# A post-norm transformer layer on one core: full-array scores, o moved by DMA, FFN bias on ScalarE, finer waits, another order of steps

## The chip, the cores and the metric

The kernel runs on one core of one Trainium2 chip. The metric is the device time of one execution in microseconds (us); less is better. A core has TensorE (PE; its weight loads are PEld), VectorE (DVE), ScalarE (ACT), GpSimd (POOL) and a queue that only issues DMAs (SP). Each engine works through its own list of instructions in order and waits on semaphores. TensorE's results land in PSUM, in banks of 128 x 512 float32; DMAs move data between HBM and SBUF and within SBUF.

## The reference, cut to what matters

```python
# x: (16, 512, 256) float32, 16 heads of 16, window blocks of 128
qkv = (x @ Wqkv + bqkv).reshape(B, S, 3, H, Dh)
scores = einsum('bhnqd,bhnkd->bhnqk', qb, kwin) / 16     # each block of 128 queries sees 3 blocks of keys
scores = where(|kpos - qpos| <= 128 and in range, scores, -1e30)
out = softmax(scores) @ vwin, reshaped to (B, S, 256)
x = layernorm(x + out @ Wout + bout)
h = relu(x @ quantize(W1).T + b1)                        # 256 -> 1024, weights -1, 0, 1
x = layernorm(x + h @ quantize(W2).T + b2)
```

## The kernel before, in words

A sequence of 512 tokens is one "row" (16 rows). The program walks `row in range(-2, B + 1)`; a step does the attention of row b, the output projection and FFN of row b-1, and the projections of row b+1. Each step has four parts v = 0..3. Part v computes the exponentials of the four heads of quad v of row b, and the row maxima of the quad that comes two parts later (quads 2 and 3 of row b, then 0 and 1 of row b+1).

**Units.** A quad has 12 units of scores and 12 of maxima. Four heads times three units: blocks of 384, of 384, and of two times 256 columns. q and k are split into a high and a low float32r part and stacked by DMAs (`stack`, six DMAs of 128 KB for a quad) into `q_stack` and `k_stack`: quads 0 and 1 lie on partitions 0 to 49, quads 2 and 3 on 64 to 113. So scores (50 partitions) and maxima (48 partitions) of the same part use different halves of the array. Scores go to banks `st_a`, `st_b`, maxima to three banks `mx`. DVE adds the band and takes the maximum (L812), transposes and a DMA bring the negated maximum into `q_stack` as two more rows (step "nmt", L518, L411). ACT takes exp (L670), POOL zeroes the outside of the band (L973, L977).

**Side steps.** The list `SIDE` says, for each part, in which order the rest is issued: "qk" j and "vp" i are projections (L484), "pva" and "pvb" multiply probabilities by v (L503; four heads in four 32-column strips of the array), "ut" transposes the result u (L513) so that DVE can divide by the sums (L848, L852), "ot" transposes it back (L543), "op" is the output projection, "ln1", "x1", "x1t" the first norm and its transpose (L564), "f1" hf p a 256-token piece of FFN 1 (L578 adds the bias as a matmul of 1 with `b1_rows`, L582 the rest), "f2" FFN 2 (L595), "ln2" the second norm, "xs" the split of x, "xr" the residual load. `weave` spreads the units over the side steps by the costs in `COST`, two units at a time (`RUN = 2`, `N_MAX = 3`). `LAG` says by how many maxima DVE puts a side step off.

**Order on SP.** A step begins with the load of x for row b+2 (L381), then `stack(b, 3)` in part 0, `stack(b+1, 0..2)` in parts 1 to 3, the residual load in part 2, `store(b, 0)` in part 3, each part's "nmt" DMA, and `store(b, 1)` at the end. `store` waits for the second norm's scaling on POOL (L1027).

Of the kernel before, what the change touches and what calls it, by code (L numbers as in the profile page):

```python
# [62 lines left out]
]  # L63

COST = {"qk": (3072, 6), "vp": (3072, 12), "op": (3072, 12), "ut": (1024, 4), "ot": (1024, 4), "x1t": (1024, 4),
        "nmt": (256, 1), "f1": (2560, 10), "f2": (8192, 32), "pva": (2200, 1), "pvb": (2200, 1)}
# [4 lines left out]
N_MAX = 3  # L71
# [4 lines left out]
N_SHARED = 6 - N_MAX  # L76

USES_BANK = {"pva", "ut", "qk", "ot", "op", "vp", "x1t", "f1", "f2", "nmt"}
# [20 lines left out]
NEEDS = {"ot": "ut", "op": "ot", "f1": "x1t", "f2": "f1"}  # L99


def weave():

    out = []
    for v in range(QUADS):
        total = sum(COST.get(name_of(s), (0, 0))[0] for s in SIDE[v])
        units = []
        for i in range(UNITS):
            pos = (i // RUN * RUN + RUNS_AT[0]) / UNITS * total * RUNS_AT[1]
            units += [(pos, "scores", i), (pos, "max", i)]  # L110
# [11 lines left out]
WOVEN = weave()  # L122

# [9 lines left out]
def row_of(v, step, at):  # L133
# [9 lines left out]
    if name == "xr":  # L143
        return (0, None) if attn else None
# [17 lines left out]
def dve_order(v):  # L162
# [7 lines left out]
    for step, woven in zip(SIDE[v], WOVEN[v]):  # L170
# [9 lines left out]
        after = late[-1][0] + 1 if late and name_of(late[-1][1]) == name_of(step) in ("ln1", "ln2") else 0  # L180
# [12 lines left out]
def postln_layer(nc, xT, x, wqkv, bqk, bv, wout, bout, w1T, b1, w2T, b2, out):  # L193
    ctx = ExitStack()
    with ctx:
# [11 lines left out]
        B1 = sb("b1_rows", [P, FF], F32R)  # L207
        ONES2 = sb("ones_rows", [P, S // 2], F32R)
# [5 lines left out]
        ONES = sb("ones", [P, P])  # L214
# [5 lines left out]
        SK = sb("k_stack", [P, 8, S], F32R)  # L220
# [4 lines left out]
        RC = sb("recip", [P, TB * 4])  # L225
        ON = sb("o_norm", [P, TB, D])
        OT = [sb("oT_hi", [P, KC, S], F32R), sb("oT_lo", [P, KC, S], F32R)]
        Y = sb("y", [P, TB, D])
        X1 = sb("x1", [P, TB, D])
        X1T = [sb("x1T_hi", [P, KC, S], F32R), sb("x1T_lo", [P, KC, S], F32R)]  # L230
        HID = [sb("hid_hi", [P, FC, S // 2], F32R), sb("hid_lo", [P, FC, S // 2], F32R)]
        RMAX = sb("rmax", [P, 4, NB])
        NMW = sb("neg_max", [P, P])
        NM = NMW[:, 0:8 * NB].rearrange("p (a g n) -> p a g n", a=2, g=4)
        NMT = sb("neg_maxT", [8 * NB, 2, W], F32R)
# [9 lines left out]
        ABS = sb("abs_sums", [P, 3])  # L245
        THR = sb("thresholds", [P, 4])
# [5 lines left out]
        PST = [bank("st_a"), bank("st_b")]  # L252
# [10 lines left out]
        W1RAW = [X1[:, :, :].rearrange(FLAT), ON[:, :, :].rearrange(FLAT)]  # L263
        W2AT = KC * 4 * D
        W2RAW = [PRF[:, W2AT + HALF_W * k:W2AT + HALF_W * (k + 1)] for k in range(2)]
        B1R = PRF[0:1, W2AT + 2 * HALF_W:W2AT + 2 * HALF_W + FF]
# [8 lines left out]
        s_small = sem("bqk_bv_in")  # L275
        s_const = sem("constants")
# [4 lines left out]
        s_b1 = sem("b1_lo_in")  # L281
# [28 lines left out]
        s_utf = sem("uT_full")  # L310
        s_rc = sem("recip_done")
        s_on = sem("o_norm_done")
        s_otf = sem("oT_full")
# [9 lines left out]
        s_rs1 = sem("ln1_rstd_done")  # L323
        s_nmr = sem("neg_mean_rstd")
        s_x1 = sem("x1_done")
# [13 lines left out]
        s_od = sem("out_stored")  # L339
# [5 lines left out]
        def _(sp):  # L345
# [5 lines left out]
            def more_weights():  # L351
# [5 lines left out]
                sp.dma_start(B1R, b1[None, :]).then_inc(s_wo, 16)  # L357
# [3 lines left out]
            def stack(r, v, first):  # L361
# [4 lines left out]
                sp.wait_ge(s_qkl, 4 * r + 2 * c + 2)  # L366
                if not first:
                    sp.wait_ge(s_stf, 12 * (4 * r - 4 + v) + 12)
                half = slice(64 * ih, 64 * ih + 64)
                heads = slice(4 * ih, 4 * ih + 4)  # L370
                for dst, j, terms in ((SQ, 2 * c, (0, 1, 0)), (SK, 2 * c + 1, (0, 0, 1))):
                    for t, part in enumerate(terms):
                        rows = slice(64 * c + 16 * t, 64 * c + 16 * t + 16)
                        sp.dma_start(dst[rows, heads, :].bitcast(F32), QK[j][part][half, :].bitcast(F32)).then_inc(s_stk[v], 16)

            def step(b, at):
# [9 lines left out]
                if at == 0:  # L386

                    sp.wait_ge(s_wsplit_l, 3)
                    sp.dma_start(B1[1:2, :].bitcast(F32), Y[0:1, :, :].rearrange("p t d -> p (t d)")) \
                        .then_inc(s_b1, 16)  # L390
                for v in range(QUADS):
# [6 lines left out]
                    if v == 2 and attn:  # L398
                        if at == 0:
                            sp.wait_ge(s_b1, 16)  # L400
                        else:
                            sp.wait_ge(s_x1, 4 * b)
# [3 lines left out]
                    if q is not None:  # L406
                        r, vq = b + q[0], q[1]
                        sp.wait_ge(s_nmt, 4 * r + vq + 1)
                        c, ih = vq // 2, vq % 2
                        rows = SQ[64 * c + 48:64 * c + 50, 4 * ih:4 * ih + 4, :].bitcast(F32)  # L410
                        sp.dma_start(rows.rearrange("a g (n q) -> a (g n) q", n=NB), NMT[:, vq % 2].bitcast(F32)).then_inc(s_nmin[vq], 16)  # L411
                if post:
                    store(b, 1)
# [222 lines left out]
        def _(act):  # L636
# [36 lines left out]
            def side_work(v, step, b, dr, vq, at):  # L673
# [408 lines left out]
```

## Time and profile before

| what | value |
|---|---|
| time, median of 3 runs | 1185.28 us (1185.11 to 1187.25) |
| the profiled execution: its own time, its span | 1187.86 us, 1186.1 us |
| mean granted TensorE clock | 0.924 |
| busy share of PE, DVE, ACT, POOL | 89%, 72%, 52%, 44% |
| one row in the steady part (589.17 to 657.44) | 68.27 us |

The span is the time from the first to the last instruction of the profiled execution; what lies around it is 1.8 us. A row repeats from about 112 us to 1067 us, from the part in which the first attention row starts to the last row that still prepares another.

### The profile page before, as it was taken

The page shows a single profiled execution, that of the slowest core. Times are in us where ns is not written, and L with a number is a line of the kernel's source. Part 1 is how long each engine was busy: PE and PEld are TensorE (multiplying, and loading weights), DVE is VectorE, ACT ScalarE, POOL GpSimd, SP SyncE. Part 2 cuts the span into 40 slices and gives each one's busy share as a digit, 9 for nine tenths or more (in the row PEclk, how much of TensorE's full clock was granted, in tenths as well). Part 3 has the DMA queues.
Part 4 walks back from the last instruction along what each step waited for, and adds up shares of the span by engine and source line. Part 5 has one row for each costly group of instructions (what it writes and reads, how often), then busy time and mean ns, then how long its engine had stood idle before and what let it go on. Part 6 is the DMA issues. An engine that isn't in the chain of part 4 may idle for free.

```text
span 1186.1 us, 23520 instructions
## 1 busy us (share of the span) xinstructions
PE 1056.2 (89%) x8132; PEld 771.9 (65%) x8132; DVE 859.3 (72%) x2934; ACT 613.3 (52%) x1258; POOL 518.8 (44%) x824
## 2 busy tenths in 40 slices
PE   4778899999989899998989999898989999897966
PEld 3444676766767576676767666676767667675755
DVE  3975777778787777778777777877777787777333
ACT  4154554655455564556455555545655554555421
POOL 2124353544535445463535445453535445344430
PEclk9677899998989999898999989898998989898889
DMA  5835255434354443444344534424554342442000
GB/s 169 108 54 92 28 82 82 68 70 73 58 75 68 83 73 76 61 80 65 56 82 73 88 61 78 75 37 82 82 82 68 69 74 57 57 69 56 1 19 18
DMA packets 56999, 81.49 MB, mean 69 GB/s; under 512 B 7729, under 2 KB 27697, under 8 KB 56882
## 3 DMA queue, kind: packets, MB, share of 16 engines
q1 hardware_dynamic: 56882, 80.00, 40.3%
q8 instruction: 66, 1.08, 0.4%
q14 instruction: 51, 0.42, 0.2%
HBM read 20.19 MB, written 8.39 MB: 24 GB/s over the span
## 4 chain that ended last, share of the span: by engine, by line
PE 77%; DVE 13%; issue 4%; POOL 2%; ACT 2%; DMA 1%; SPq 0%; POOLq 0%; DVEq 0%; ACTq 0%
PE shared L484 18%; PE st_a L459 13%; PE shared L503 12%; PE shared L595 11%; PE shared L582 10%; DVE mx L812 5%; PE st_b L459 5%; PE shared L578 3%; PE shared L564 3%; DVE oT_lo L859 2%; POOL ln_rstd L1007 1%; PE shared L543 1%; PE mx L475 1%; DVE qk_lo L839 1%; DVE rmax L812 1%
## 5 line engine op out<-in xcount | busy, mean ns | idle before, releaser
L812 DVE CUSTOM_DVE_ANT_0 mx<-mx,band 128x384 f32<-128x384 f32 (+1 forms) x1024 | 480.1, 514 | 187.0 <-PE mx L475 182.6
L670 ACT ACTIVATE probs<-st_a 128x384 f32<-128x384 f32 (+1 forms) x384 | 202.0, 526 | 371.3 <-PE st_a L459 367.7
L475 PE MATMUL mx<-k_stack,q_stack 48*128 48x384 f32 (+1 forms) x1024 | 273.0, 369 | 8.0 <-DMA k_stack<-qk_lo 3.9
L973 POOL TENSOR_SCALAR_AFFINE_SELECT probs<-probs 128x512 f32<-128x512 f32 (+1 forms) x256 | 128.8, 527 | 317.5 <-ACT probs L670 316.3
L670 ACT ACTIVATE probs<-st_b 128x384 f32<-128x384 f32 (+1 forms) x384 | 200.8, 523 | 0.0
L459 PE MATMUL st_a<-q_stack,k_stack 50*128 50x384 f32 (+1 forms) x512 | 186.9, 406 | 3.1 <-ACT probs L670 2.4
L475 PEld LDWEIGHTS mx<-k_stack,q_stack 48*128 48x128 f32 x1024 | 165.7, 201 | 13.2 <-DVE rmax L812 8.7
L503 PE MATMUL shared<-probs,v_aug 128*32 128x384 f32 (+1 forms) x2048 | 161.2, 445 | 0.7 <-DVE x L902 0.7
L459 PEld LDWEIGHTS st_a<-q_stack,k_stack 50*128 50x128 f32 x512 | 90.3, 197 | 104.2 <-issue 63.5
L812 DVE DVE_READ_ACCUMULATOR2_ANT rmax<- 128x1 f32 x1024 | 144.5, 141 | 0.0
L459 PE MATMUL st_b<-q_stack,k_stack 50*128 50x384 f32 (+1 forms) x512 | 143.2, 320 | 0.0
L582 PE MATMUL shared<-x1T_hi,w1q 128*128 128x256 f32 x512 | 142.9, 295 | 0.0
L582 PE MATMUL shared<-x1T_lo,w1q 128*128 128x256 f32 x512 | 138.5, 288 | 0.0
L595 PE MATMUL shared<-w2q,hid_hi 128*128 128x256 f32 x512 | 131.9, 293 | 4.1 <-DVE hid_lo L895 4.1
L595 PE MATMUL shared<-w2q,hid_lo 128*128 128x256 f32 x512 | 131.8, 293 | 0.0
L977 POOL TENSOR_SCALAR_AFFINE_SELECT probs<-probs 128x512 f32<-128x512 f32 (+1 forms) x256 | 127.1, 520 | 0.0
L895 DVE SCALAR_TENSOR_TENSOR hid_lo<-shared,hid_hi 128x512 fp32r<-128x512 f32 x128 | 87.9, 687 | 36.0 <-ACT hid_hi L740 34.6
L740 ACT ACTIVATE hid_hi<-shared 128x512 fp32r<-128x512 f32 x128 | 76.8, 600 | 59.4 <-PE shared L582 59.4
L595 PEld LDWEIGHTS shared<-w2q,hid_hi 128*128 128x128 f32 x512 | 97.7, 191 | 14.7 <-issue 10.2
L582 PEld LDWEIGHTS shared<-x1T_hi,w1q 128*128 128x128 f32 x512 | 99.4, 194 | 10.5 <-issue 7.7
L503 PEld LDWEIGHTS shared<-probs,v_aug 128*32 128x32 f32 x2048 | 57.7, 111 | 68.2 <-issue 50.7
L595 PEld LDWEIGHTS shared<-w2q,hid_lo 128*128 128x128 f32 x512 | 97.4, 190 | 6.9 <-issue 2.9
(107 smaller groups left out, 1965.3 us busy)
## 6 DMA issues: line engine op xcount, KB each, us to landing
q_stack<-qk_hi SPq DMA_DIRECT2D x128, 128.0 KB, 4.3
k_stack<-qk_hi SPq DMA_DIRECT2D x128, 128.0 KB, 5.2
x_raw<-in_xT SPq DMA_DIRECT2D x16, 512.0 KB, 5.7
q_stack<-qk_lo SPq DMA_DIRECT2D x64, 128.0 KB, 3.9
k_stack<-qk_lo SPq DMA_DIRECT2D x64, 128.0 KB, 5.5
y<-in_x SPq DMA_DIRECT2D x16, 512.0 KB, 6.1
out<-x SPq DMA_DIRECT2D x32, 256.0 KB, 2.1
probs<-in_w2T SPq DMA_DIRECT2D x1, 1024.0 KB, 10.6
```

Of the source, the lines that this page charges most:

```text
L459: mm = pe.matmul(PST[i % 2][:, col:col + n], SK[rows, hd, W * m:W * m + W], SQ[rows, hd, q0:q0 + n], start=True, stop=True)
L475: mm = pe.matmul(PMX[i % N_MAX][:, col:col + n], SQ[rows, hd, W * m:W * m + W], SK[rows, hd, k0:k0 + n], start=True, stop=True)
L484: mm = pe.matmul(ps, lhs(a, kc), rhs(z, kc), start=(n == 0), stop=(n == len(terms) - 1))
L503: mm = pe.matmul(G[32 * g:32 * g + 32, q0:q0 + width], VAUG[:, vq, m, g, :], PR[:, vq % 2, g // 2, lo:lo + width], start=(m == 0), stop=(m ...
L582: mm = pe.matmul(ps, W1Q[:, kc, P * f:P * f + P], X1T[a][:, kc, 256 * hf:256 * hf + 256], start=False, stop=(kc == KC - 1 and a == 1))
L595: mm = pe.matmul(G[:, D * t:D * t + D], HID[a][:, f, P * t:P * t + P], W2Q[:, f, :], start=(f == 0 and a == 0), stop=(f == FC - 1 and a == 1))
L670: act.activation(PR[:, v % 2, g // 2, lo:lo + n], PST[i % 2][:, 0:n], ACT.Exp, scale=SCALE) \
L740: act.activation(HID[0][:, 2 * p:2 * p + 2, :].rearrange("p f t -> p (f t)"), G[:, :], ACT.Relu).then_inc(s_hh, 1)
L812: mx = dve.tensor_tensor_reduce(ps, ps, band, 1.0, -3e38, ALU.add, ALU.max, RMAX[:, g, m:m + 1])
L895: dve.scalar_tensor_tensor(pair[1], G[:, :], 0.0, pair[0].bitcast(F32), ALU.max, ALU.subtract).then_inc(s_hl, 1)
L973: pool.affine_select(out=pr_before, in_=pr_before, compare_op=ALU.is_ge, fill=0.0, base=0, pattern=[[0, n], [1, W]], channel_multiplier=-1)
L977: last = pool.affine_select(out=pr_after, in_=pr_after, compare_op=ALU.is_ge, fill=0.0, base=0, pattern=[[0, n], [-1, W]], channel_multipl ...
```

## The change

- **Scores and maxima use the whole array.** `k_stack` becomes two tensors, one for quads 0 and 1 and one for 2 and 3, each zero in the other half's partitions; `q_stack` is shared. Scores multiply 128 partitions, maxima 112. The two rows of ones and the negated maximum move to partitions 124 to 127. A `stack` now waits also for the maxima of two quads earlier, and scores for the stack of the quad two later. `BANKS = (2, 3)` gives two banks for scores and three for maxima, as before; the "nmt" transpose (72 columns of output) uses a bank of the maxima.
- **o goes to columns by DMA.** "ut" and "ot" on TensorE go. v is interleaved with ones, so that u holds o on even and the sum on odd partitions. `columns`, two DMAs of 128 KB for a quad, bring them apart into `o_cols` and `sums_cols`; step "od" takes the reciprocal of 128x512 sums and multiplies (half 0: reciprocal on DVE, product on POOL; half 1: both on DVE). "ot" is then the split of `o_cols` on ACT and DVE.
- **FFN bias on ScalarE.** The matmul L578 goes. ACT applies bias and relu in two 256-column instructions to `u` or `hidden` (by turns), then copies to float32r; DVE or, for p = 1, POOL subtracts.
- **Waits.** op, x1t, f1 and f2 wait for the half, tile or pair that they need, the first norm's scale is computed for two tiles at a time, x1 tiles 0 and 2 are on DVE, 1 and 3 on ACT.
- **Order.** A new `SIDE`, new costs, single units instead of pairs, and some ACT steps ahead of the exponentials of their step.

```diff
 SIDE = [
-    [("qk", 0), "nmt", "pva", "pvb", ("vp", 0), "ut", ("vp", 1), ("ot", 0), ("ot", 1), ("qk", 1), ("op", 0),
-     ("op", 1)],
-    [("ln1", 0), ("ln1", 1), ("ln1", 2), ("qk", 2), "nmt", ("ln1", 3), "pva", "pvb", ("x1", 0), ("x1", 1),
-     ("x1", 2), ("x1", 3), "ut", ("x1t", 0), ("x1t", 1), ("qk", 3), ("f1", 0, 0)],
...
+    [("ot", 0), ("qk", 0), ("qk", 1), "pva", "pvb", "nmt", ("vp", 0), ("qk", 2), ("od", 1)],
+    [("qk", 3), ("ot", 1), ("vp", 1), ("op", 0), ("ln1", 0), ("ln1", 1), ("op", 1), ("ln1", 2), ("ln1", 3), "nmt",
+     ("x1", 0), ("x1", 1), ("x1", 2), "pva", "pvb", ("xs", 0), ("x1", 3), ("x1t", 0), ("x1t", 1), ("f1", 0, 0),
+     ("f1", 0, 1)],
+    [("f1", 0, 2), ("f1", 0, 3), "pva", "pvb", "nmt", ("f2", 0)],
+    [("xs", 1), ("f1", 1, 0), "nmt", "xr", ("ln2", 0), ("f1", 1, 1), ("ln2", 1), ("f1", 1, 2), ("f1", 1, 3),
+     ("od", 0), "pva", "pvb", ("f2", 1), ("ln2", 2), ("ln2", 3)],
 ]
-RUN = 2
-RUNS_AT = (0.5, 0.92)
-LAG = {"ln1": 1, "ln2": 1, "qk": 1, "ot": 1, "x1t": 0, "f1": 0, "op": 1, "ut": 0, "f2": 1}
+BANKS = (2, 3)
+N_SCORE, N_MAX = BANKS
+REST_ON_POOL = (1,)
+X1_ON_DVE = (0, 2)
+LAG = {"ln1": 1, "ln2": 0, "qk": 0, "od": 3, "ot": 0, "x1t": 0, "f1": 2, "op": 0, "f2": 1}
...
             def scores(b, v, i, at):
-                rows = slice(64 * c, 64 * c + 50)
                 if i == 0:
                     pe.wait_ge(s_stk[v], 96 * b + 96)
                     pe.wait_ge(s_nmin[v], 16 * b + 16)
+                    if v < 2 or stages(at)[2]:
+                        pe.wait_ge(s_stk[(v + 2) % 4], 96 * (b + v // 2) + 96)
...
-                    mm = pe.matmul(PST[i % 2][:, col:col + n], SK[rows, hd, W * m:W * m + W],
-                                   SQ[rows, hd, q0:q0 + n], start=True, stop=True)
+                    mm = pe.matmul(PST[i % N_SCORE][:, col:col + n], SK[c][:, hd, W * m:W * m + W],
+                                   SQ[:, hd, q0:q0 + n], start=True, stop=True)
...
+            def columns(r, vq):
+                i, q = vq // 2, 4 * r + vq
+                rows = slice(64 * (vq % 2), 64 * (vq % 2) + 64)
+                sp.wait_ge(s_u, q + 1)
...
+                sp.dma_start(OC[rows, i, :], U[0:P:2, :]).then_inc(s_uin, 16)
+                sp.dma_start(SC[rows, :], U[1:P:2, :]).then_inc(s_uin, 16)
...
+                elif name == "od":
+                    i = step[1]
+                    dve.wait_ge(s_uin, 128 * r + 64 * i + 64)
+                    dve.reciprocal(SC[:, :], SC[:, :]).then_inc(s_rc, 1)
+                    if i == 1:
+                        dve.wait_ge(s_rc, 2 * r + 2)
+                        dve.tensor_tensor(OC[:, i, :], OC[:, i, :], SC[:, :], ALU.mult).then_inc(s_od, 1)
...
-                        pe.matmul(ps, B1[:, P * f:P * f + P], ONES2[:, :], start=True, stop=False)
...
+                    if p % 2 == 0:
+                        act.wait_ge(s_uin, 32 * min(4 * b + v - (SIDE[v].index(step) < SIDE[v].index("pvb")), 4 * B))
+                    if n > 1:
+                        act.wait_ge(*rest_done(n - 2))
+                    for k, f in enumerate((2 * p, 2 * p + 1)):
+                        last = act.activation(H[:, 256 * k:256 * k + 256], G[:, 256 * k:256 * k + 256], ACT.Relu,
+                                              bias=B1C[:, f:f + 1])
+                    last.then_inc(s_hr, 1)
+                    act.wait_ge(s_hr, n + 1)
+                    act.activation(HID[0][:, 2 * p:2 * p + 2, :].rearrange("p f t -> p (f t)"), H[:, :],
+                                   ACT.Identity).then_inc(s_hh, 1)
```

## Rows read from the trace of the kernel before

**Rows 1.** The page: span, busy time (share of the span) of the engines.

```profile
span 1186.1 us, 23520 instructions
PE 1056.2 (89%) x8132; PEld 771.9 (65%) x8132; DVE 859.3 (72%) x2934; ACT 613.3 (52%) x1258; POOL 518.8 (44%) x824
```

**Rows 2.** Windows: length, busy of PE, PEld, DVE, ACT, POOL, clock, DMA share, GB/s.

```profile
589.17:657.44 68.27, 63.51 (x511) 46.67 (x510) 52.61 (x183) 37.73 (x78) 32.50 (x52) 0.95 0.40 72
...
615.00:617.00 2.00, 0.74 (x5) 0.44 (x5) 1.57 (x9) 1.12 (x3) 1.02 (x2) 1.00 0.02 1
617.00:619.00 2.00, 0.60 (x5) 0.31 (x3) 1.76 (x7) 1.18 (x3) 1.85 (x6) 0.69 0.00 0
619.00:621.00 2.00, 1.94 (x9) 1.65 (x11) 0.76 (x4) 1.26 (x3) 0.77 (x2) 0.50 0.00 0
```

**Rows 3.** Waits in one row's length (560 to 628 us): total, times, longest.

```profile
PE shared L564 <- ACT x L727: 1.5, 1, 1.5
PE shared L513 <- ACT u L714: 1.4, 1, 1.4
...
PE shared L484 <- DVE o_norm L852: 1.0, 1, 1.0
...
PE shared L484 <- DVE oT_lo L859: 0.6, 1, 0.6
```

**Rows 4.** Timeline of PE: runs of units in FFN 2 and at part 1, nmt, pv.

```profile
586.71 0.28 PE L595 MATMUL shared<-w2q,hid_hi 128*128 128x256 f32 x1
586.92 0.44 PE L459 MATMUL st_a<-q_stack,k_stack 50*128 50x384 f32 x1
586.92 0.44 PE L475 MATMUL mx<-k_stack,q_stack 48*128 48x384 f32 x1
...
587.75 0.28 PE L595 MATMUL shared<-w2q,hid_hi 128*128 128x256 f32 x1
...
592.76 0.39 PE L484 MATMUL shared<-xT_lo,wqkv_hi 128*128 128x512 f32 x1
592.99 0.27 PE L518 MATMUL shared<-identity,neg_max 128*128 128x128 f32 x1
593.20 1.28 PE L503 MATMUL shared<-probs,v_aug 128*32 128x256 f32 x16
...
609.26 0.44 PE L459 MATMUL st_a<-q_stack,k_stack 50*128 50x384 f32 x1
```

**Rows 5.** Pieces of the chain that ended last (start, length).

```profile
560.52 0.12 PE shared L578
...
601.55 0.87 PE shared L543 x8
```

**Rows 6.** Timeline of DVE, then of POOL, from the end of FFN 2.

```profile
589.38 0.68 DVE L902 TENSOR_TENSOR x<-shared,x 128x512 f32<-128x512 f32 x1
589.98 0.24 DVE L848 RECIPROCAL recip<-shared 128x16 f32<-128x16 f32 x1
...
590.60 0.74 DVE L910 BATCH_NORM_STATS2 ln_stats<-x 128x6 f32<-128x256 f32 x2
...
591.66 0.19 POOL L1020 TENSOR_SCALAR var_eps<-ln_mv 128x2 f32<-128x2 f32 x1 [1.28 <-DVE ln_mv L913]
591.93 0.72 POOL L1022 TENSOR_TENSOR ln_rstd<-var_eps,minus_half 128x2 f32<-128x2 f32 x1
592.76 2.43 POOL L1027 TENSOR_SCALAR x<-x,ln_mv,ln_rstd 128x256 f32<-128x256 f32 x2
```

**Rows 7.** Timeline of SP's issues, then DMA sizes and time to landing.

```profile
595.22 0.39 SPq L417 DMA_DIRECT2D out<-x  x1
...
599.55 0.67 SPq L374 DMA_DIRECT2D k_stack<-qk_lo  x1
...
k_stack<-qk_lo SPq DMA_DIRECT2D x1, 128.0 KB, 6.6
...
k_stack<-qk_lo SPq DMA_DIRECT2D x1, 128.0 KB, 5.0
```

More of the change, by code:

```diff
@@ L106, in weave @@
         total = sum(COST.get(name_of(s), (0, 0))[0] for s in SIDE[v])
[L107 to L110, printed above, removed]
+        units = [((i + SCORES_AT[0]) / UNITS * total * SCORES_AT[1], "scores", i) for i in range(UNITS)]
+        units += [((i + MAXIMA_AT[0]) / UNITS * total * MAXIMA_AT[1], "max", i) for i in range(UNITS)]
+        units.sort()
         at, slot = 0, []
@@ L122, with units_before, ffn_steps_in_u @@
 WOVEN = weave()
+def units_before(v, step, kind):
+    return sum(k == kind for woven in WOVEN[v][:SIDE[v].index(step)] for _, k, _ in woven)
+NMT_AT = [units_before(v, "nmt", "max") for v in range(QUADS)]
+assert max(NMT_AT) < UNITS
+def ffn_steps_in_u():
+    out, n, last = [], 0, 0
+    for v in range(QUADS):
+        for step in SIDE[v]:
+            if name_of(step) == "f1":
+                n += 1
+                last = n if step[2] % 2 == 0 else last
+            if step == "pvb":
+                out.append(last)
+    return out
+U_FFN = ffn_steps_in_u()
 def stages(at):
@@ L213, in postln_layer @@
         IDN = sb("identity", [P, P])
[L214 removed]
+        ONES = ONES2[:, :].bitcast(F32)
         BAND = sb("band", [P, 3 * W])
@@ L466, in max_scores @@
                 c, hd = v // 2, 4 * (v % 2) + g
-                rows = slice(64 * c, 64 * c + 48)
+                rows = slice(0, 112)
                 if i == 0:
@@ L471, in max_scores @@
                     pe.wait_ge(s_mxr, 12 * (4 * r + v) + i - N_MAX + 1)
+                if i == NMT_AT[(v + 2) % 4] and not (first and v == 0):
+                    pe.wait_ge(s_nmt, 4 * r + v)
                 for m in BLOCKS[u]:
@@ L483, in split3 @@
                     passed()
+                    if chunk is not None and n % 3 == 0:
+                        chunk(kc)
                     mm = pe.matmul(ps, lhs(a, kc), rhs(z, kc), start=(n == 0), stop=(n == len(terms) - 1))
@@ L751, in step @@
                             other_weights()
+                        row = row_of(v, step, at)
+                        before = name_of(step) in ("nmt", "ot", "pvb", "x1")
+                        if row is not None and before:
+                            side_work(v, step, b, *row, at)
                         for _, kind, i in woven:
@@ L754, in step @@
                                 exp(b, v, i, at)
-                        row = row_of(v, step, at)
-                        if row is not None:
+                        if row is not None and not before:
                             side_work(v, step, b, *row, at)
@@ L871, in side_work @@
                         dve.wait_ge(s_mv2, 4 * r)
-                        dve.wait_ge(s_x1, 4 * r)
+                        for t in range(TB):
+                            dve.wait_ge(*x1_done(r - 1, t))
                     t = step[1]
@@ L890, in side_work @@
                         .then_inc(s_x1l, 1)
-                elif name == "f1":
+                elif name == "f1" and step[2] not in REST_ON_POOL:
                     hf, p = step[1], step[2]
@@ L959, in _ @@
             pool.memset(ONES2[:, :].bitcast(F32), 1.0).then_inc(s_const, 1)
-            pool.memset(B1[:, :].bitcast(F32), 0.0).then_inc(s_const, 1)
-            pool.memset(SK[:, :, :].bitcast(F32), 1.0).then_inc(s_const, 1)
+            for half in SK:
+                pool.memset(half[:, :, :].bitcast(F32), 0.0).then_inc(s_const, 1)
             pool.wait_ge(s_const, CONSTANTS)
```

296 lines of the change are left out of this document (156 added, 140 removed), and 4 rows, old and new, of the table SIDE.

## The prediction

> **What bounds the kernel now.** I read the page first: PE is busy for 89% of the span and the next engine, DVE, for 72% [rows 1]. Then the windows, cut to one row in the steady part: of 68.27 us PE works 63.51 and DVE 52.61, so neither is full, and for some 6.8 us of each row the clock is at its lower level, 1.2 instead of 2.4 GHz [rows 2] (the slice from 617 us has 0.69 of full speed, the one from 619 has 0.50, and it stays so until nearly 625). Then the waits, to see what PE's 4.8 idle us of a row are: 1.5 for x1, 1.4 for u, 1.0 for o_norm, 0.6 for oT_lo [rows 3], the rest small. The clock falls just after the wait for x1, where PE was busy 0.74 and 0.60 of 2 us [rows 2]. PE then worked about 5.4 us at half speed, which cost 2.7 us. So a row is PE work at full clock of 60.8 us, idle time of 4.8 and 2.7 of low clock. PE bounds the kernel, and the waits that count are the ones that end on it.
>
> **PE's work.** *Scores and maxima.* A row has 24 runs of two units. From the last FFN matmul ahead of a run to the second one behind it 1.04 us pass (586.71 to 587.75) [rows 4], two of them the usual 0.12 apart: 0.80 us for the run. It starts each score matmul at the time of its twin for the maxima, so a run pays once for two matmuls. But its 896 columns, at the 0.118 us that an FFN matmul of 256 takes, are 0.41 us of it; 0.39 us go into the passage from full-array matmuls to these and back. A transpose (L518) among full-array matmuls costs no such gap (592.99 is 0.23 behind 592.76), the column strips of L503 behind it do (593.20, 0.21 later where the transpose needs 0.11) [rows 4]: the gap belongs to the change of tile, not to a wait. 24 runs at 0.80 to 0.85 (the latter where a unit of 384 columns follows another) are 19.2 to 20.4; I take 19.6 us. In the full array nothing is doubled and nothing switches: 0.118 us for 256 columns and 0.233 for 512 [rows 4], halfway 0.175 for 384; four blocks, twice, for 16 heads are 18.7 us. So -0.9 us.
> The Trainium skill (TensorE: Matmul & The Clock Gate, Part 3: Packing small matmuls) says that small matmuls in distinct row groups run together and that this is the gain to go for; by that rule alone the change would double 9.35 us a row. It also says (TensorEngine Tiling (Array Packing), Key Properties) that a change of tiling mode drains the array, and the trace's 0.39 us a run agrees.
> *Bias.* 16 matmuls of 0.118 [rows 5]: -1.9. *u and o transposes.* 16 and 8 of 0.109 (0.87 for eight) [rows 5]: -2.6. Together PE's work falls by 5.4 us a row. I keep -5.4; the least is -4.4 (no gain on the units, u's transposes partly in the shadow of the switch), the most -6.4.
>
> **PE's idle time.** The waits for u, o_norm and oT_lo go (3.0 us): the path of o has qk 2, qk 3 and vp 1 in front of it. Two places remain or are new.
> *The start of part 1.* Call S the end of f2 (589.17). The last stack of q and k for a row, quad 3, is issued in part 0 and needed by the first unit of part 1. Its path is not touched: z at S+0.2; its 0.60, then norm statistics, now without the division between them (-0.62); POOL from var_eps to the end of the scaling 3.5 us [rows 6]; so the store is issued at S+5.4 instead of 6.05, then x, six stack transfers, the last at S+9.8, landing 6.6 us later [rows 7]: S+16.4. Now PE comes there at S+20.1 (609.26) [rows 4]. After the change part 0 has no op, vp 1, ut and ot: three qk (18 at 0.233, 4.2), vp 0 (12 at 0.118, 1.4), two halves of pv (1.28 each [rows 4] and their borders, 2.8), nmt 0.1, a quarter of 18.7: 13.2 us, so PE arrives at S+13.4 and waits 3.0 us. If the transfers land as fast as those of the emptier queue (5.0 us [rows 7]) it is 1.4; with the negated maximum's DMA landing 1.5 us behind, 4.5. Then "od" 1: `columns` is issued after it (SP needs 0.67 us for an issue [rows 7]), lands at about S+17.8, DVE stands at the head of its queue until then, with every later maximum behind it, and takes 1.3 us for reciprocal and product (a 128x512 operation is 0.60 apart, as L902 [rows 6]; bounds 0.5 to 1.5 each). The first maximum is then read at S+19.6; the fourth, which needs its bank, is due at S+19.9: no wait.
> *x1.* Call T the end of op 1. y 0.6, statistics 1.0, POOL 0.2+0.3+0.7+0.2 with the steps between, then ACT with u, an exp and xs 0 ahead in its queue: the last tile of x1 is there at T+5.4. PE has pv, three unit pairs and three transposes, to T+4.4: 1.0 idle. Then x1T's halves with nothing behind them (qk 3 stood there before): ACT 0.6 and DVE 0.7, 1.3 idle. Together 2.3 instead of 1.5. Bounds 1 and 4.
> With 0.6 for small ones (now 0.3) idle is 5.9: +1.1.
>
> **Clock.** The fall now at x1 costs 2.7. x1's wait becomes two shorter ones with work between; the wait at part 1 is one of 3.0 us, longer than the one that today precedes the fall. I take one low stretch, moved to part 1: 0. Bounds: none (-2.7), both (+2.7).
>
> **Beside the path.** ACT: 8 times two 256-column relus instead of one of 512, a wait for itself and a copy, +0.7 each, to 43.5 of 64 us. DVE: without ut (2.7) and one of four 128x512 subtractions (1.2), with two reciprocals and a product (1.9), 50.5. POOL +4, to 37. SP: 8 issues more, 5 us of a row. All have room on average; what they delay is in the rivals. In the prologue the memset of a second k_stack ends before the first qk input; the tail gains 2 us of bias and loses as much in transfers for o. Row 15 has no maxima beside its scores and waits for the same stack: no change.
>
> **Sum.** -5.4 + 1.1 + 0 = -4.3 us a row; 15 rows (-1 to 14 count as 15 whole ones): -65. The profiled span of 1186.1 becomes 1121, its execution 1123; the median lay 2.6 below the profiled execution, so **1121**.
>
> **Rivals.**
> (a) *Both low stretches.* The two short waits of x1 (2.3 us within 2.9) bring the clock down as well: +2.7 a row, 1162. For it: the slices before today's fall were busy for a third only [rows 2]; mine would be so for 2.9 us. Together with a landing 1.5 us later it reaches 1183.
> (b) *No wait at part 1.* If the six transfers land by S+14.5 or PE is later than I count, the wait shrinks below a microsecond and the clock stays up there: -2 to -3 for the wait, -2.7 for the clock, 1040 to 1095. Against it: these transfers share the engines with x (512 KB).
> (c) *Slower: transfers of u.* `columns` adds 1 MB of SBUF traffic a row, in the queue behind the stack. Where "od" 1 waits on DVE, each microsecond that it lands after S+18 is one that all maxima and PE's banks wait. It must be 4.5 us later, S+22.3, to eat the gain, and then slower with (a): 1190 to 1215. Against it: DMA engines are used for 40% of the row [rows 2].
> (d) *Slower: the rule of row groups.* If the 0.39 us of a run stay (each single unit still pays for something at its borders) while the twins come apart, 24 x 0.39 = 9.4 us a row more than counted: 1262. The transpose without a gap [rows 4] speaks against it. This is what the skill's rule on row groups would bring.
> (e) *Nothing.* Idle time grows by what PE's work loses: 1183 to 1188.
>
> **Numbers.** Forecast (1095 to 1145) 0.38; (a) 1145 to 1183 0.20; (b) 0.27; (c) 0.08; (d) 0.04; (e) 0.03. 0.2% is about what a measurement of this kernel can tell from no change. Faster is the forecast, (a) and (b), 0.85; same 0.03; slower 0.12. The range from 1045 to 1183 leaves out 0.07 below and 0.13 above; the forecast's own is 1095 to 1145.
>
> **What would show it.** Right: in steady rows score and maxima matmuls of 128 and 112 rows about 0.175 apart, units with no gap at their borders, a row of 64 us, PE waiting for a stack or a maximum at the first unit of part 1 for 3 us, the low clock behind it, DVE idle ahead of the reciprocal, x1's wait split in two. Wrong: full clock throughout and a row under 60 us (b), two low stretches (a), PE waiting for DVE's maxima in part 1 (c), units dearer than 0.8 us for two pairs (d). Most doubtful is the arrival time at part 1: it sets the wait and the clock together.

## The result

The changed kernel takes 1277.53 us (median of 4 runs, 1275.92 to 1282.52), the kernel before beside it 1186.26 us (4 runs, 1185.11 to 1187.25): ratio 1.0777, 95% interval 1.0744 to 1.0809. It is 7.8% slower; I had forecast 1121 us and a range from 1045 to 1183.

The page of the changed kernel: span and busy times, then the chain that ended last, by engine and by line.

```profile
span 1275.8 us, 23049 instructions
PE 1055.8 (83%) x7492; PEld 842.3 (66%) x7492; DVE 940.1 (74%) x2821; ACT 736.4 (58%) x1513; POOL 630.1 (49%) x936
...
PE 47%; DVE 20%; DMA 11%; ACT 7%; issue 7%; SPq 7%; POOL 1%; DVEq 0%; POOLq 0%; ACTq 0%
```

PE has 640 matmuls less than before and is as long busy as before [rows 1], in a longer span. Less than half of the chain is PE's; DVE has 20% and transfers 11%.

One row in the steady part, then windows of 2 us at three places (columns as in [rows 2]).

```profile
573.00:648.40 75.40, 64.27 (x468) 51.70 (x468) 56.49 (x174) 45.53 (x94) 39.40 (x58) 0.95 0.45 78
...
618.00:620.00 2.00, 0.32 (x1) 0.32 (x2) 2.00 (x8) 0.00 (x0) 1.05 (x1) 0.94 0.00 0
620.00:622.00 2.00, 2.00 (x11) 2.00 (x11) 1.77 (x10) 0.88 (x2) 0.42 (x2) 0.50 0.18 66
...
640.00:642.00 2.00, 0.00 (x0) 0.00 (x0) 0.00 (x0) 0.00 (x0) 0.00 (x0) 1.00 1.15 139
...
644.00:646.00 2.00, 2.00 (x8) 1.72 (x7) 0.92 (x1) 0.54 (x3) 0.00 (x0) 0.50 1.08 121
...
650.00:652.00 2.00, 2.00 (x11) 1.81 (x11) 2.00 (x7) 1.38 (x3) 0.00 (x0) 0.62 0.01 4
652.00:654.00 2.00, 2.00 (x11) 2.00 (x11) 1.29 (x6) 0.49 (x1) 0.00 (x0) 0.53 0.03 8
```

A row is 75.40 us where 68.27 were [rows 2] and 64 were forecast. It has two low stretches of the clock (0.50 in the windows from 620 and from 644), each behind a stop of PE: from 618 to 620 PE is busy for 0.32 us while DVE works throughout, from 640 to 642 no engine works at all, while the DMA engines are full. Just behind this row, after another stop of PE, the clock is low again (0.62 and 0.53 in the last two windows).

Waits of that row (total, times, longest), which answer to [rows 3].

```profile
PEld mx L546 <- DVE rmax L888: 6.7, 8, 2.0
...
PE mx L546 <- DMA k_stack_bottom<-qk_lo: 3.8, 1, 3.8
...
PE mx L546 <- DVE rmax L888: 2.9, 3, 1.8
...
PE mx L546 <- ACT neg_maxT L768: 1.8, 2, 1.1
...
PE shared L642 <- DVE oT_x1T_lo L959: 1.1, 1, 1.1
...
PE shared L628 <- ACT x L791: 0.6, 1, 0.6
...
PE shared L557 <- DVE oT_x1T_lo L928: 0.4, 1, 0.4
```

The waits for u and o_norm are gone, the one for the split of o (L928) is 0.4 and the one for x1 is 0.6. In their place PE waits for the stack of quad 3 and, in weight loads and matmuls, for DVE to read maxima.

PE's timeline in part 3 and at the start of part 1, then DVE's (start, length, operation, in brackets the idle time before it).

```profile
615.60 0.28 PE L656 MATMUL shared<-w2q,hid_hi 128*128 128x256 f32 x1
615.71 0.34 PE L546 MATMUL mx<-k_stack_top,q_stack 112*128 112x384 f32 x1
615.88 0.34 PE L528 MATMUL st<-q_stack,k_stack_bottom 128*128 128x384 f32 x1
616.06 0.28 PE L656 MATMUL shared<-w2q,hid_lo 128*128 128x256 f32 x1
...
617.60 0.28 PE L656 MATMUL shared<-w2q,hid_lo 128*128 128x256 f32 x1
619.68 0.77 PE L546 MATMUL mx<-k_stack_top,q_stack 112*128 112x256 f32 x2 [1.80 <-DVE rmax L888]
...
638.19 0.40 PE L557 MATMUL shared<-xT_hi,wqkv_hi 128*128 128x512 f32 x1
642.43 0.44 PE L546 MATMUL mx<-k_stack_bottom,q_stack 112*128 112x384 f32 x1 [3.84 <-DMA k_stack_bottom<-qk_lo]
...
649.75 0.44 PE L546 MATMUL mx<-k_stack_bottom,q_stack 112*128 112x384 f32 x1 [1.72 <-DVE rmax L888]
```

```profile
615.51 3.35 DVE L921 RECIPROCAL sums_cols<-sums_cols 128x512 f32<-128x512 f32 x1
618.78 0.41 DVE L888 CUSTOM_DVE_ANT_0 mx<-mx,band 128x256 f32<-128x256 f32 x1
...
645.08 3.35 DVE L921 RECIPROCAL sums_cols<-sums_cols 128x512 f32<-128x512 f32 x1 [1.12 <-DMA sums_cols<-u]
648.47 0.69 DVE L924 TENSOR_TENSOR o_cols<-o_cols,sums_cols 128x512 f32<-128x512 f32 x1
649.08 0.56 DVE L888 CUSTOM_DVE_ANT_0 mx<-mx,band 128x384 f32<-128x384 f32 x1
```

The reciprocal over 128x512 takes 3.35 us, in both halves of o (x32, 107.2 us in all). I had put 0.6 on it. Its neighbour, a product of the same shape, takes 0.69. While the reciprocal runs no maximum is read, PE fills its three banks and stops: at 617.88 (until 619.68), and in part 1 at 648.03 (until 649.75).

SP's issues around the start of part 1, then the time from issue to landing in that window, which answer to [rows 7].

```profile
629.51 0.38 SPq L485 DMA_DIRECT2D out<-x  x1
629.93 0.47 SPq L433 DMA_DIRECT2D x_raw<-in_xT  x1
630.56 0.61 SPq L426 DMA_DIRECT2D q_stack<-qk_hi  x1
...
633.77 0.63 SPq L426 DMA_DIRECT2D k_stack_bottom<-qk_lo  x1
...
635.91 0.60 SPq L481 DMA_DIRECT2D sums_cols<-u  x1
...
k_stack_bottom<-qk_lo SPq DMA_DIRECT2D x1, 128.0 KB, 8.6
...
sums_cols<-u SPq DMA_DIRECT2D x1, 128.0 KB, 9.1
```

The last stack transfer lands 8.6 us after its issue, at 642.4, and the sums at 645.06, 9.1 after theirs. The same transfers for quad 2 take 5.5 us, those of the sums in the other parts 2.9 (medians over the rows). Here x, the stack, the columns of u and the next stack follow each other within 11 us.

### The profile page after: what moved, and what is told of

Same layout as the page of the kernel before. It is cut to its first block, busy times and chain, and to the rows that moved or that the text cites. A ratio compares the mean times of both kernels' runs of the same rounds, so it can differ in the third digit from the quotient of the medians.

```text
span 1275.8 us, 23049 instructions
## 1 busy us (share of the span) xinstructions
PE 1055.8 (83%) x7492; PEld 842.3 (66%) x7492; DVE 940.1 (74%) x2821; ACT 736.4 (58%) x1513; POOL 630.1 (49%) x936
## 3 DMA queue, kind: packets, MB, share of 16 engines
q1 hardware_dynamic: 68136, 96.84, 43.2%
## 4 chain that ended last, share of the span: by engine, by line
PE 47%; DVE 20%; DMA 11%; ACT 7%; issue 7%; SPq 7%; POOL 1%; DVEq 0%; POOLq 0%; ACTq 0%
PE shared L576 11%; DMA sums_cols<-u 9%; PE mx L546 9%; DVE sums_cols L921 8%; PE shared L642 8%; PE st L528 7%; PE shared L656 6%; PE shared L557 6%; DVE mx L888 5%; SPq L426 4%; ACT u L811 2%; DVE oT_x1T_lo L928 1%; ACT hidden L811 1%; DVE x L972 1%; ACT u L776 1%
## 5 line engine op out<-in xcount | busy, mean ns | idle before, releaser
L730 ACT ACTIVATE probs<-st 128x384 f32<-128x384 f32 (+1 forms) x768 | 394.1, 523 | 317.8 <-PE st L528 314.6
L546 PE MATMUL mx<-k_stack_bottom,q_stack 112*128 112x384 f32 (+1 forms) x512 | 162.3, 359 | 90.4 <-DMA k_stack_bottom<-qk_lo 49.2
L546 PE MATMUL mx<-k_stack_top,q_stack 112*128 112x384 f32 (+1 forms) x512 | 153.3, 346 | 52.2 <-DVE rmax L888 31.4
L642 PE MATMUL shared<-oT_x1T_hi,w1q 128*128 128x256 f32 x512 | 140.2, 296 | 16.7 <-DVE oT_x1T_lo L959 16.0
L528 PE MATMUL st<-q_stack,k_stack_top 128*128 128x384 f32 (+1 forms) x512 | 150.6, 336 | 3.3 <-DMA q_stack<-neg_maxT 2.5
L528 PE MATMUL st<-q_stack,k_stack_bottom 128*128 128x384 f32 (+1 forms) x512 | 144.5, 323 | 3.3 <-ACT probs L730 2.0
L642 PE MATMUL shared<-oT_x1T_lo,w1q 128*128 128x256 f32 x512 | 139.6, 292 | 0.0
L921 DVE RECIPROCAL sums_cols<-sums_cols 128x512 f32<-128x512 f32 x32 | 107.2, 3349 | 25.0 <-DMA sums_cols<-u 25.0
L642 PEld LDWEIGHTS shared<-oT_x1T_hi,w1q 128*128 128x128 f32 x512 | 102.6, 200 | 20.5 <-issue 20.5
L528 PEld LDWEIGHTS st<-q_stack,k_stack_top 128*128 128x128 f32 x512 | 97.2, 209 | 10.7 <-issue 7.0
L642 PEld LDWEIGHTS shared<-oT_x1T_lo,w1q 128*128 128x128 f32 x512 | 102.9, 201 | 0.0
```

Of the source, the lines that this page charges most:

```text
L528: mm = pe.matmul(PST[i % N_SCORE][:, col:col + n], SK[c][:, hd, W * m:W * m + W], SQ[:, hd, q0:q0 + n], start=True, stop=True)
L546: mm = pe.matmul(PMX[i % N_MAX][:, col:col + n], SQ[rows, hd, W * m:W * m + W], SK[c][rows, hd, k0:k0 + n], start=True, stop=True)
L642: mm = pe.matmul(G[:, 256 * k:256 * k + 256], W1Q[:, kc, P * f:P * f + P], X1T[a][:, kc, 256 * hf:256 * hf + 256], start=(kc == 0 and a == ...
L730: act.activation(PR[:, v % 2, g // 2, lo:lo + n], PST[i % N_SCORE][:, 0:n], ACT.Exp, scale=SCALE) \
L921: dve.reciprocal(SC[:, :], SC[:, :]).then_inc(s_rc, 1)
```

## Experiments

Each time is the median beside runs of the kernel before on the same chip (1185.5 to 1187.9 us there); differences are against 1277.5 us unless another kernel is named. "A row" is a sixteenth.

### The reciprocal and the place of the stack

**No reciprocal.**
```diff
-dve.reciprocal(SC[:, :], SC[:, :]).then_inc(s_rc, 1)
+dve.tensor_scalar(SC[:, :], SC[:, :], 1.0, None, ALU.mult).then_inc(s_rc, 1)
```


> The changed kernel with each 128x512 reciprocal on DVE (3.35 us, two a row) replaced by a multiplication by 1.0 in the same place. It leaves the reciprocal out: o is multiplied by the sums instead of being divided by them. Theory A (the reciprocal was priced at 0.6 us and takes 3.35; it stands in DVE's queue ahead of the maxima, once for each half of o, and PE waits for both): if the replacement takes about 0.55 us, 2.8 us go from each of two places a row, 16 rows, 90 us: 1188 us, with 1170 to 1215 as the bounds. Theory B (the landing of the last transfers decides the start of part 1, and the reciprocal mostly fills time in which PE waits anyway): no more than one of the two places gives something back, at most 45 us, 1232 or above.

Measured: 1202.7 us (ratio to before 1.0134, 1.0100 to 1.0169), 75 us less, 4.7 a row for 5.4 us of DVE work taken away (the multiplication takes 0.43 us at the end of part 0, but 0.86 in part 3). Theory A's range held; B fell. It is still slower than before, so the reciprocal isn't all.

**One half at a time**, the same edit for `i == 0` or `i == 1` alone.

> The changed kernel, with the reciprocal of the first half of o alone (in part 3) replaced by the multiplication by 1.0; this leaves that reciprocal out. With both replaced 75 us went. If the two places cost alike, 1240 us (1230 to 1250). If the place at the end of part 0 carries it (there PE first waits for the stack, then for the maxima behind the reciprocal), 1260 us or more here and 1215 or less in the run beside it; if part 3 carries it, the reverse.

> The same for the second half of o alone (end of part 0). Two places that cost alike: 1240 us (1230 to 1250). The place at the end of part 0 alone: 1215 us or less. The place in part 3 alone: 1260 us or more, since the wait for the stack and for the transfers of u is still there.

Measured: 1230.5 us without the one in part 3 (47 us less), 1247.0 without the one at the end of part 0 (31 less). Both lie within the bounds of "alike" (1230 to 1250), at its two ends, and the executions of the two kernels do not overlap (1228 to 1234 and 1239 to 1251). So both reciprocals are on the path, and together they make 78, the 75 of both. The one that my forecast never put on the path, in part 3, is the dearer, although less DVE work went there.

**Stack first.** In SP's queue the stack of quad 3 goes ahead of the store and of x:
```diff
 attn, post, nxt, nxt2 = stages(at)
+if attn:
+    stack(b, 3, at == 0)
+if at >= 2:
+    store(b - 1, 1)
 if nxt2:
...
-    if v == 0 and attn:
-        stack(b, 3, at == 0)
...
-if post:
+if at == B:
     store(b, 1)
```


> The changed kernel with one order changed in SP's queue: the stack of quad 3 is issued first in a step, ahead of the store of the second half of the row before and of the load of x. Reciprocals stay. In the profile of the changed kernel PE waits 3.8 us for this stack at the start of part 1 and the transfers of u behind it land 9.2 us after their issue. The stack can now be issued about 5 us earlier. Theory A (the reciprocal decides): the wait for the stack goes, but DVE still stands before the transfers of u and then 3.35 us in the reciprocal; at most the 3.8 us are given back in each of 15 rows, so 1220 to 1277 us, with 1240 as the likeliest. Theory B (transfers decide): both the stack and the transfers of u land 4 us or more earlier, 1200 us or below.

Measured: 1226.3 us (1.0322, 1.0302 to 1.0342), 51 us less, within theory A's bounds; theory B fell. PE's wait for this stack, 49.2 us over all rows, is 0.5. Its wait for maxima is what is left:

```profile
PEld mx L548 <- DVE rmax L890: 140.5, 143, 5.0
...
PE mx L548 <- DVE rmax L890: 74.8, 45, 4.8
```

**x behind the stack, the store still in front**, to see which of the two held it up:
```diff
+if attn:
+    stack(b, 3, at == 0)
 if nxt2:
```
(and the line in the loop removed, the store unchanged at the end of a step).

> The changed kernel with only the load of x (512 KB) moved behind the stack of quad 3 in SP's queue; the store stays in front, and SP waits there for the end of the second norm. Theory T1 (the load of x shares the DMA engines with the stack, whose last transfer took 8.6 us to land): the landing comes down to 5 or 6 us, about 3 us a row, 1225 to 1240 us, nearly all that the stack first brought. Theory T2 (the wait for the store, until 5.4 us into the part, sets the landing): only the issue of x, 0.7 us a row, is gained, 1262 to 1277 us.

Measured: 1261.0 us, 16.5 less, just beyond T2's range and far from T1's. The landing did what T1 said: the last stack transfer took 5.5 us (median over the rows) instead of 8.1, and with x behind the stack PE's wait for it fell from 49.2 to 7.2 us. But the transfers behind it now share with x: the sums still take 6.7 us to land at this place (8.6 before), and 26 us of wait for the negated maximum (2.5 before) took a good part of the stack's place. The rest of the 51 us, 35, came only with the store behind the stack too.

**Both edits**, no reciprocal and stack first.

> Both edits of the two runs before together: the multiplication by 1.0 in the place of the reciprocal (the reciprocal is left out) and the stack of quad 3 issued first in a step. If the two costs are the two terms by which the forecast of 1121 us was wrong, and nothing else was, this run should come to about that: 90 us for the reciprocals and 40 to 55 for the stack from 1277, 1130 to 1150 us. If it stays above 1180, something else that neither theory names holds at least 2 us of each row.

Measured: 1123.4 us (0.9456, 0.9431 to 0.9480), 154 us less than the changed kernel and 5.4% faster than before, 7 us below the range expected. Together the two edits give more than the sum of their own runs (75 + 51): with one cost gone, part of its time goes into waits for the other (PE's wait for maxima rose from 61.4 to 74.8 us with the stack first, its wait for the stack from 49.2 to 51.9 without the reciprocals). Without these two costs the change is a gain, so nothing else is needed to explain the loss.

### Can the reciprocal be hidden on DVE?

```diff
-    [("ot", 0), ("qk", 0), ("qk", 1), "pva", "pvb", "nmt", ("vp", 0), ("qk", 2), ("od", 1)],
-    [("qk", 3), ("ot", 1), ("vp", 1),
+    [("ot", 0), ("qk", 0), ("qk", 1), "pva", "pvb", "nmt", ("vp", 0), ("qk", 2)],
+    [("od", 1), ("qk", 3), ("vp", 1), ("ot", 1),
...
-    [("xs", 1), ("f1", 1, 0), "nmt", "xr", ("ln2", 0), ("f1", 1, 1), ("ln2", 1), ("f1", 1, 2), ("f1", 1, 3),
-     ("od", 0), "pva",
+    [("xs", 1), ("f1", 1, 0), "nmt", "xr", ("ln2", 0), ("od", 0), ("f1", 1, 1), ("ln2", 1), ("f1", 1, 2), ("f1", 1, 3),
+     "pva",
...
+cols = slice(S // RECIPS * k, S // RECIPS * (k + 1))
+dve.reciprocal(SC[:, cols], SC[:, cols]).then_inc(s_rc, 1)
```
with the stack first, `RECIPS` 4 in one run and 1 in the other.

> The order of the last pair of runs (the stack of quad 3 first in a step) with the true reciprocal, cut into four pieces of 128 columns that stand in DVE's queue with a maximum between two of them: for the first half of o in part 3 from the statistics on, for the second half at the start of part 1 instead of the end of part 0. Theory A (what costs is how long a single block keeps the maxima from being read, PE having three banks for them): a piece is about 0.85 us, less than the banks give, so the 103 us between the run with the stack first (1226) and the one without reciprocals (1123) come back but for a few: 1125 to 1155 us. Theory C (what costs is DVE's total, 5.8 us more a row on an engine that is busy for 52.5 of 65 us): the time stays near 1226 us, 1195 or above.

> The same places in DVE's queue as the run before, but each reciprocal whole (128x512, 3.35 us) instead of in four pieces. Theory A (length of the block against three banks): maxima come about 1.3 us apart, so PE waits some 1.5 to 2.5 us in each of two places a row, 1165 to 1215 us. Theory P (only the old places were bad, the end of part 0 above all): within 10 us of the run with four pieces.

Measured: 1279.4 us in quarters and 1239.9 whole. Theory A fell in both runs and P in the second; of C only the bound (1195 or above) held, not the 1226 itself. Finer pieces were the slower. Waits of the kernel in quarters, over all rows:

```profile
PE shared L563 <- DVE oT_x1T_lo L938: 81.5, 16, 11.5
...
ACT hidden L817 <- POOL hid_lo L1098: 52.7, 15, 3.5
...
PE st L534 <- ACT probs L736: 43.7, 26, 3.5
```

PE no longer stops for maxima, but for what the later reciprocal delays: op waits about 4.6 us of a steady row for the second half of o, and POOL, which waits at the head of its queue for the sums of the first half (52.6 us over all rows, 26.3 in the changed kernel), holds back hid_lo, which ScalarE waits for, and so the exponentials. Four pieces also cost more than one (128 of 0.935 us, 118 us, for 107). At the start of part 1 DVE has no room: in the run with both edits it works from 569.74 to 578.7 with hardly a gap.

**Off DVE.** Stack first, and ScalarE makes the reciprocal:
```diff
+act.preload_act_table_set("natural_log_exp_and_others")
...
+act.wait_ge(s_uin, 128 * r + 64 * i + 64)
+act.activation(SC[:, :], SC[:, :], ACT.Ln).then_inc(s_ln, 1)
+act.wait_ge(s_ln, 2 * r + i + 1)
+act.activation(SC[:, :], SC[:, :], ACT.Exp, scale=-1.0).then_inc(s_rc, 1)
...
-dve.wait_ge(s_uin, 128 * r + 64 * i + 64)
-dve.reciprocal(SC[:, :], SC[:, :]).then_inc(s_rc, 1)
```


> The stack of quad 3 first in a step, and the reciprocal of the sums taken off DVE: ScalarE computes exp(-ln(s)) in its place, two 128x512 activations of about 0.6 us for each half of o, with both functions in the one table set that is loaded at the start. Theory A' (the two runs before showed that a piece at the start of part 1 or in part 3 costs wherever DVE, or a helper that waits for it, has no slack; what counts is that these 6.7 us leave DVE at those places): this should come near the run without reciprocals (1123 us), 1125 to 1145. Rival: ScalarE stands at the head of its queue for the transfers of u and then 1.2 us in the two activations, PE has only two banks for scores, and two such waits a row cost 1 to 2 us each: 1150 to 1190 us.

Measured: 1128.3 us (0.9512, 0.9488 to 0.9537), as theory A' had it. It beats both kernels, by 4.9% and 11.7%. One row of it, its waits in that row, and the new instructions:

```profile
565.00:630.00 65.00, 60.53 (x476) 48.89 (x472) 51.43 (x174) 47.10 (x99) 39.36 (x59) 1.00 0.51 94
```

```profile
PE mx L549 <- ACT neg_maxT L772: 1.8, 2, 1.1
PE shared L645 <- DVE oT_x1T_lo L967: 1.1, 1, 1.1
PE shared L631 <- ACT x L801: 0.6, 1, 0.6
PE mx L549 <- DVE rmax L898: 0.2, 1, 0.2
PE st L531 <- ACT probs L734: 0.2, 1, 0.2
PE shared L560 <- DVE oT_x1T_lo L936: 0.2, 1, 0.2
```

```profile
L786 ACT ACTIVATE sums_cols<-sums_cols 128x512 f32<-128x512 f32 x32 | 20.2, 632 | 1.0
L784 ACT ACTIVATE sums_cols<-sums_cols 128x512 f32<-128x512 f32 x32 | 19.8, 619 | 8.5 <-DMA sums_cols<-u 8.5
...
L701 ACT ACT_TABLE_LOAD x1 | 1.3, 1283 | 0.8 <-PEq L1164 0.8
```

0.62 and 0.63 us instead of 3.35, on an engine with room, and no wait in a row is over 1.1 us, so the clock stays up. The Trainium skill (ScalarE: Activation LUTs, Table sets: the hidden batching unit) says that one set holds exp and ln together; the single table load agrees.

### The terms of PE's work

**Maxima in a row group.**
```diff
-rows = slice(0, 112)
+rows = slice(64 * c, 64 * c + 48)
```


> The changed kernel with the maxima's matmuls cut to the 48 rows of one half of the array (what they leave out are rows that hold zeros, so the result is unchanged), while the scores keep all 128 rows. Each unit of maxima is then a passage from the full array to another tile and back, with no twin that could share it. By the step of my forecast that put 0.39 us on such a passage in the kernel before, 48 units a row cost up to 18.7 us more a row where PE is not waiting, up to 280 us in all, and at least a half of that where PE's waits hide some: 1400 to 1560 us. If the change of tile costs nothing and the kernel before lost its 0.39 us to something else, the time stays at 1277 us.

Measured: 1483.2 us in a single execution, 206 more, 12.9 a row or 0.27 for each of 48 passages, within the range expected. In FFN 2 of this kernel a pair of units and its borders:

```profile
644.00 0.28 PE L656 MATMUL shared<-w2q,hid_hi 128*128 128x256 f32 x1
644.21 0.44 PE L546 MATMUL mx<-k_stack_top,q_stack 48*128 48x384 f32 x1
644.58 0.44 PE L528 MATMUL st<-q_stack,k_stack_bottom 128*128 128x384 f32 x1
644.86 0.28 PE L656 MATMUL shared<-w2q,hid_lo 128*128 128x256 f32 x1
```

0.86 us from the first start to the last, where the changed kernel has 0.46 for the same four matmuls (615.60 to 616.06, above). So a way to the other tile and back costs 0.40 us, where I took 0.39, and in the full array it is gone. Over the run less of it shows (0.27), for PE waits less: 4.8 us for the stack instead of 49.2, 43.2 for maxima instead of 61.4.

**The bias alone**, in the kernel before: the bias matmul goes, ScalarE does two relus with a bias into a buffer and a copy. Then the same with f2's waits per pair of tiles.
```diff
-pe.matmul(ps, B1[:, P * f:P * f + P], ONES2[:, :], start=True, stop=False)
...
+for k, f in enumerate((2 * p, 2 * p + 1)):
+    last = act.activation(H32[p % 2][:, 256 * k:256 * k + 256], G[:, 256 * k:256 * k + 256],
+                          ACT.Relu, bias=B1C[:, f:f + 1])
```


> The kernel before with one part of the change alone: the FFN bias is added on ScalarE (two 256-column relus with a bias into a buffer, then a copy) and the 16 bias matmuls of a row are gone. By my forecast's term 1.9 us of PE work go from each of 16 rows and ScalarE's 0.7 us more for each of 8 pieces lie beside the path: 1187 minus 30, 1150 to 1165 us. Rival: hid_lo, for which PE already waited a little, comes 1 us later at the head of both f2 in a row, and takes 1 to 2 of the 1.9 us back: 1170 to 1187 us.

> The kernel before with the FFN bias on ScalarE, as in the run that gave 1215 us, and in addition f2's waits for hid_hi and hid_lo taken per pair of tiles instead of all at its start, as the change has them. In that run PE waited 43 us for hid_lo at f2, 4 in the kernel before. Theory W (that wait, and nothing else, turned the 30 us of saved bias work into a loss): about 39 us come back and part of a low stretch of the clock, 1155 to 1180 us. Theory E (ScalarE's longer pieces delay the exps and the maxima's banks too, wherever the waits stand): 1195 us or above.

Measured: 1215.4 us (1.0238, 1.0216 to 1.0260) and 1208.0 us (1.0186, 1.0153 to 1.0220). 1.9 to 2.4% slower than the kernel before, beyond my rival's range and with theory W refuted (theory E's bound held). Of the first kernel, over all rows:

```profile
PE st_a L452 <- DVE hid_lo L891: 35.9, 13, 2.8
...
PE mx L468 <- DVE rmax L808: 11.5, 18, 1.7
```

Hidden values come later (0.47 + 0.47 + 0.63 us on ScalarE for 0.60), and PE waits for them at f2. With waits per tile that wait is gone and others stand in its place: 22.2 us for maxima and 21.8 for exponentials. In the order of the kernel before, the longer pieces on ScalarE cost more than the 30 us of matmuls that they save.

**The bias matmuls put back** into the fastest kernel, as 16 matmuls a row that are overwritten, and **each maxima matmul twice** in it.

> The fastest kernel so far (1128 us: stack first, exp(-ln) on ScalarE) with 16 more matmuls of 256 columns a row, one ahead of each group of FFN 1, whose result is overwritten by the next; the bias stays on ScalarE. It puts back what the change took off PE and nothing else. If my term of 1.9 us a row is right and PE sets the row there, 30 us more: 1150 to 1165 us. If the place of the bias matmuls lies beside the path (PE waits anyway for ScalarE or DVE near FFN 1), less than 15 us more, up to 1143.

> The fastest kernel with each maxima matmul issued twice into the same bank (the second overwrites the first with the same values), 64 more full-array matmuls a row. At the prices of my forecast (0.175 us for 384 columns, 0.118 for 256, half of each) they cost 9.4 us a row, 16 rows, 150 us: 1278 us, if PE sets every stretch and a full-array unit has no cost besides its columns. Below 1250 us: PE has slack at a good part of the units, and work taken off it there is not given back in full either. Above 1300 us: a unit costs more than its columns.

Measured against 1128.3: 1148.7 (20.5 more, 1.3 a row for 1.9 us of work) and 1231.2 (103 more, 6.4 a row for 9.4). The first lies between its two ranges, near the one for full price; the second is below 1250, the sign of slack. Twice the same answer: about two thirds of the added work show in the time, and a third falls where PE would have waited. The same holds for the 16 matmuls if they are taken off again; for the step from the kernel before, whose order is another, it is not shown.

**Units in runs of two** in the fastest kernel (`i // 2 * 2` for `i` in the places of the units).

> The fastest kernel (1128 us) with the units woven in runs of two maxima and two scores, as the kernel before has them, instead of single ones. In that kernel the 64 maxima matmuls and 64 score matmuls of a row take 20.3 us from start to start where my forecast had 18.7, with intervals of 0.25 to 0.28 us beside other work where 0.12 to 0.18 are usual. Theory B (each border between units and other matmuls costs something in the full array as well): half the borders, 1 us less a row, 1110 to 1120 us. Theory K (two score banks and three for maxima are the limit: PE waits for the exponentials or the maxima inside a run): 1135 us or above.

Measured: 1158.0 us, 30 more, theory K: PE's wait for DVE to read maxima rises from 9.4 to 31.1 us. With two score banks and three for maxima, single units are the better choice; what a border costs by itself this run can't tell.

## Why the prediction was wrong

**Where a row is longer than forecast.** The forecast's row of 64.0 us was 55.4 of PE's work, 5.9 of idle time and 2.7 for the low clock. For the changed kernel I added up the intervals between the starts of PE's matmuls over three rows (497.6 to 723.8 us), without the idle time and scaled by the granted clock: an estimate of 60.2 us of work a row, 10.7 of idle time and 4.5 for the clock, together 75.4. The same tally gives 60.7, 4.8 and 2.8 for the kernel before. So idle time, and the low clock behind it, made the kernel slower than before. Of the 11.4 us by which the row is longer than forecast, idle time is 4.8, PE's work, whose gain did not come, another 4.8, and the clock 1.8.

**The first step that failed** is in "The start of part 1": that DVE "takes 1.3 us for reciprocal and product (a 128x512 operation is 0.60 apart, as L902; bounds 0.5 to 1.5 each)". The product measured 0.69, the reciprocal 3.35, outside its bounds, and while it runs PE stops. I took the price of an addition for it, and the only reciprocal in the trace (128x16, 0.24 us [rows 6]) looked as cheap as any small operation. The two sizes now give (3.35 - 0.24) / (512 - 16) = 6.3 ns a column. The Trainium skill (VectorE: DVE Perf Modes, First, the fixed hardware budget) says that Reciprocal runs an iterative divide with a repeat count of 8. These runs show that it is dear, but not the count: it takes 4.9 times as long as the product of the same shape (0.69), and 7.8 or 3.9 times as long as the multiplication (0.43 or 0.86). That it is not priced like an addition stood there to be read.

**The same error beside the path.** I put the two reciprocals and the product at 1.9 us in DVE's total (7.4 measured) and said that all engines have room on average. The first half's reciprocal, in part 3, I followed no further. Alone it cost 47 us, the second 31.

**The landing.** With S the end of f2, 623.45: the store was issued at S+6.1 (5.4 forecast), the last stack transfer at S+10.3 (9.8), landing at S+18.9 (16.4). PE came at S+15.1 (13.4) and waited 3.8 us: forecast 3.0, bounds 1.4 to 4.5. This wait held, in part by luck: the transfers landed 2.5 us late and PE came 1.7 us late. What follows it did not hold: the sums landed at S+21.6 (17.8), and the first maximum was read at S+25.6 (19.6). Rival (c) had this mechanism and its bound, S+22.3; the landing came within 0.7 us of it, and the longer reciprocal did the rest. I held the two causes apart and gave (c) 0.08.

**The clock.** One low stretch was forecast, behind the wait for the stack, and it came (0.50 from 644). The stops that the reciprocals make brought others: in part 3 (0.50 from 620) and in part 1, right behind this row (0.62 and 0.53 from 650). Rival (a), a low stretch at x1, did not come in this row, where x1's wait was 0.6 and x1T's 1.1, 1.7 for 2.3; in the next row the clock falls there too (0.53 in the window from 664).

**The second step that failed: PE's work.** The forecast took 5.4 us of work off each row. By its own accounting the fastest kernel's row is 65.0 us less 4.5 of idle time (PE is busy for 60.53), no low clock, so 60.5, where before it was 60.8: 0.3 us off. The bias matmuls and transposes did go; by the tally above they had 5.3 us, more than the 4.5 forecast. But scores and maxima with their borders, which were to cost 0.9 less, cost about 5 more: their matmuls alone rise from 14.0 to 21.5 us, and what the others give back at their borders is 2.3. Most intervals do stand at the prices of the forecast, so the change of tile is gone, and rival (d) with its 0.39 us a run is out as a mechanism. Yet the 340 matmuls outside pv lie 4.3 us a row above these prices: 1.8 right behind waits, 0.7 ahead of the column strips of pv, the rest about 0.1 us at a time. That term I had put at nothing. What causes these last ones is open.

Two things besides are about waiting, not work: a third of PE work that is put back is hidden in waits, and the bias on ScalarE lengthened a chain that, in the kernel before, cost more than its matmuls.

**A sum that agrees by chance.** Without the reciprocals' cost and with the stack first the time is 1123 us, 2 from the forecast. But its row of 64.85 us is 3.4 shorter than before mainly by the clock (one low stretch of 3.4 us in two rows where there were 6.8 us in each: about 1.9 of the 2.7 us) and by idle time (4.1 for 4.8); PE's work gave under 1 us. The forecast had 5.4 from the work, nothing from the clock, and more idle time.

## What to carry to other kernels

Price an operation by its own row, and if the trace has it at one small size only, don't take another operation's price for the large one: this reciprocal cost about five times an addition of the same shape (3.35 us against 0.69), and the bound has to allow for it. Follow every long instruction on an engine that frees another's buffers, not only the one beside the wait under study, and ask whether another engine has the function. Check a gain in PE's work against a row of the new kernel: here it was nearly nothing, and a good total hid it. When a queue starts its transfers behind a wait, look at what else can go in front: moving six transfers ahead of one store and one load gave 51 us.

## What the runs showed of the hardware

A reciprocal on DVE costs 6.3 ns a column; cut in four, a piece of 128 columns takes 0.935 us. ln and exp of the same 128x512 on ScalarE take 1.25 us together. Behind a 512 KB load, the last of six stack transfers took 8.6 us to land and the sums of u 9.1, against 5.5 and 2.9 at other places; with the load behind the stack the two took 5.5 and 6.7. A way from the full array to 48 rows and back cost 0.40 us between FFN matmuls, and 0.27 over the run when every maxima unit made it.
